# The first attention groups' rows turned, split and maximised inside the head stage of a two-layer cross-attention and expert kernel

## The reference, cut to what matters

```python
kv_dca = (y_dca @ Wkv_dca + bkv_dca)...      # last 16 context rows: own keys and values
q = _ln((x @ Wq + bq).reshape(b, s1, H, HD), qn_w, qn_b)
kv = concatenate([y_main @ Wk + bk, y_main @ Wv + bv], axis=-1).reshape(b, s2, H, 2 * HD)
k = _ln(kv[..., :HD], kn_w, kn_b);  v = kv[..., HD:]
ctx = _attn(q, k, v) + _attn(q, k_dca, v_dca)  # two softmaxes: over 496 keys and over 16
return ctx @ Wo + bo
```

## Time and profile before

| | us |
|---|---|
| median of 3 runs (2388.86 to 2392.63) | 2389.5 |
| profiled execution, its own time | 2395.94 |
| its span | 2394.2 |
| TensorE busy | 1989.2 (83%) |
| VectorE busy | 1155.8 (48%) |
| GpSimd busy | 1141.4 (48%) |
| ScalarE busy | 543.5 (23%) |

### The profile page before, as it was taken

One profiled execution on the slowest core, in us unless ns is written; L12 is line 12 of the kernel. 1 busy time (PEld: TensorE's weight loads), 2 busy tenths in 40 slices (PEclk: granted clock), 3 DMA queues, 4 the chain that ended last, 5 costly groups with the idle time before them and its releaser, 6 DMA issues.

```text
span 2394.2 us, 33404 instructions
## 1 busy us (share of the span) xinstructions
PE 1989.2 (83%) x10468; PEld 1422.6 (59%) x10469; DVE 1155.8 (48%) x2197; ACT 543.5 (23%) x1151; POOL 1141.4 (48%) x566
## 2 busy tenths in 40 slices
PE   5946887969854889999589999999999999999910
PEld 3424443424322333333379999999999999999810
DVE  2564442057673566774773444444444554443300
ACT  3221221101112444443112221122222122222100
POOL 0000000003562455563435557667666878781886
PEclk8977997979985789999789999999999999999965
DMA  3051004121125346711124435554555545543999
GB/s 111 0 147 61 18 27 162 58 80 49 63 83 174 117 163 226 237 51 41 40 88 162 182 118 167 174 159 152 161 163 163 176 160 188 177 163 90 207 158 196
DMA packets 199485, 305.96 MB, mean 128 GB/s; under 512 B 16472, under 2 KB 94808, under 8 KB 199416
## 3 DMA queue, kind: packets, MB, share of 16 engines
q1 hardware_dynamic: 141624, 187.24, 24.8%
q0 software_dynamic: 21504, 50.93, 9.4%
q10 hardware_dynamic: 36288, 66.84, 7.9%
HBM read 186.42 MB, written 118.55 MB: 127 GB/s over the span
## 4 chain that ended last, share of the span: by engine, by line
PE 41%; POOL 5%; DVE 2%; DMA 1%; issue 1%; POOLq 0%; ACT 0%; DVEq 0%
PE psum L2230 16%; PE psum L2250 8%; PE psum L2235 8%; POOL X L1954 5%; PE psum L2255 4%; PE psum L2217 3%; PE psum L2224 2%; DMA X<-d_y,f_slots 1%; DVE f_arena L1175 1%; DVE e_gu_low L2144 0%; DVE f_arena L1165 0%; DVE f_arena L1174 0%; DVE f_arena L1183 0%; DVE e_gu_low L2079 0%; POOLq L1791 0%
## 5 line engine op out<-in xcount | busy, mean ns | idle before, releaser
L2230 PE MATMUL psum<-e_gu_high,e_rowT_high 128*128 (+1 forms) x1272 | 428.0, 339 | 6.3 <-DVE e_gu_low L2144 3.8
L2230 PE MATMUL psum<-e_gu_low,e_rowT_high 128*128 (+1 forms) x1272 | 408.6, 323 | 0.0
L2235 PE MATMUL psum<-e_gu_high,e_rowT_low 128*128 (+1 forms) x1272 | 256.1, 323 | 22.0 <-DVE e_rowT_low L2034 22.0
L1973 ACT ACTIVATE e_silu<-psum 128x352 f32<-128x352 f32 x159 | 73.7, 464 | 879.4 <-PE psum L2235 873.9
L2230 PEld LDWEIGHTS psum<-e_gu_high,e_rowT_high 128*128 128x128 f32 x1272 | 240.7, 189 | 31.1 <-issue 27.0
L2230 PEld LDWEIGHTS psum<-e_gu_low,e_rowT_high 128*128 128x128 f32 x1272 | 241.6, 190 | 3.8
L2235 PEld LDWEIGHTS psum<-e_gu_high,e_rowT_low 128*128 128x128 f32 x1272 | 213.7, 189 | 22.3 <-DVE e_rowT_low L2034 22.3
L2045 DVE TENSOR_TENSOR e_midT_low<-psum,e_midT_high 128x256 fp32r<-128x256 f32 x159 | 67.5, 424 | 325.6 <-ACT e_midT_high L1982 323.4
L2250 PE MATMUL psum<-e_d_high,e_midT_high 128*128 (+3 forms) x477 | 187.7, 394 | 1.0 <-ACT e_midT_high L1982 1.0
L2250 PE MATMUL psum<-e_d_low,e_midT_high 128*128 (+3 forms) x477 | 188.4, 395 | 0.0
L1954 POOL DMA_INDIRECT X<-d_y,f_slots x96 | 148.1, 1542 | 83.3 <-DVE f_arena L2065 52.8
(11 more groups left out here) (348 smaller groups left out, 3787.6 us busy)
## 6 DMA issues: line engine op xcount, KB each, us to landing
d_sorted<-f_hs SPq DMA_DIRECT2D x32, 1048.0 KB, 9.6
e_row<-d_sorted ACTq DMA_DIRECT2D x125, 262.0 KB
d_y<-f_arena ACTq DMA_DIRECT2D x127, 256.0 KB
f_gu_in<-in_L_ffn_w_gate SPq DMA_DIRECT2D x32, 704.0 KB, 5.2
f_gu_in<-in_L_ffn_w_up SPq DMA_DIRECT2D x32, 704.0 KB, 5.1
f_d_in<-in_L_ffn_w_down SPq DMA_DIRECT2D x32, 512.0 KB
d_y<-f_hs SPq DMA_DIRECT2D x8, 1024.0 KB, 5.7
f_d_in<-in_L_ffn_w_down SPq DMA_DIRECT2D x32, 192.0 KB
```

Source lines behind the costliest of these rows:

```text
L2230: nc.tensor.matmul(bank[:, 0:M].unsqueeze(1), rowT_high[par][:, k, :], w[:, bass.ds(buffer, 1), k, at:at + M], start=(k == 0 and n == 0), ...
L2235: last = nc.tensor.matmul(bank[:, 0:M].unsqueeze(1), rowT_low[par][:, k, :], gu_high[:, bass.ds(buffer, 1), k, at:at + M], start=False, st ...
```

## The change

A new class `Scores` holds what the attention stage's preparation needs (the row tiles inside `f_gu_in` and `f_d_in`, high, low and exact tiles, `sel`, the maxima's tile of even groups, and 14 semaphores), and its methods are the old local functions. It is made ahead of `project_heads`, so that both stages can use it.

In the head stage, SyncE loads `sel` behind the affine rows, and the rows of groups 0 and 1 (both of batch 0) once it has issued batch 1's stores. In batch 3, VectorE first clears group 0's maxima and casts `sel`; TensorE turns group 0's q rows behind kv tile 1 and its k rows behind tile 2, and group 1's rows behind the first two scores; ScalarE splits group a's rows behind each of the two squares; GpSimd makes group 0's low parts ahead of the power of k and group 1's behind it; VectorE finds three maxima of group 0 between the scaling of q and that of k, and five behind it. In every batch b_o is now added to X behind the scaling of q instead of ahead of the sum of k's squares, and the keys and values are made straight from `ctxT`, without the copy `x_ctx_b`. GpSimd's loop over the batches is written out.

In the attention stage, the loads, turns, splits, low parts, scores and maxima ahead of the group loop are gone, as is the load of `sel`; VectorE clears the maxima's tile of odd groups only.

```diff
--- before.py
+++ after.py
...
+class Scores:
+
+
+    KINDS = ("q", "k")
+    PAIRS = 2 * JT
+
+    def __init__(self, nc, c, stack):
+        self.nc, self.c = nc, c
+        gu_flat = c.gu_in[:].rearrange("p k n -> p (k n)")
+        self.row = [gu_flat[:, n * 2 * S:(n + 1) * 2 * S].rearrange("p (a j d) -> p a j d", a=2, j=JT) for n in range(2)]
+        self.exact = [gu_flat[:, 4 * S:5 * S], c.d_in[:, 0, :]]
+        self.high = [far_sbuf(nc, stack, f"y_{a}_high", [P, 3, S], F32R) for a in self.KINDS]
+        self.low = [far_sbuf(nc, stack, f"y_{a}_low", [P, 3, S], F32R) for a in self.KINDS]
+        self.sel = far_sbuf(nc, stack, "y_sel", [P, 2, P], F32R)
+        self.nmax = [c.d_in[:, 2, :].rearrange("p (j n) -> p j n", j=JT)]
+        made = [nc.alloc_semaphore("y_" + n) for n in (
+            "rows_even rows_odd q_turned k_turned q_high k_high q_exact k_exact q_low k_low shifted scored max_ready sel_ready").split()]
+        self.rows_loaded, self.turned, self.high_ready, self.exact_ready, self.low_ready = [made[2 * n:2 * n + 2] for n in range(5)]
+        self.shifted, self.scored, self.max_ready, self.sel_ready = made[10:]
+        self.of_stage = made
+        self.first, self.at = c.bank[6], 4
+
+    def load_rows(self, sp, g):
+        b, hc = g // (X_H * X_HD // P), g % (X_H * X_HD // P)
+        for kind, name in enumerate(("d_xq", "d_xk")):
+            sp.dma_start(self.row[kind][:, g % 2], self.c.dram[name][b, :, hc * P:(hc + 1) * P].rearrange("(j p) d -> p j d", p=P)).then_inc(
+                self.rows_loaded[g % 2], 16)
+...
+    def find_max(self, dve, g, n):
+        dve.wait_ge(self.scored, g * self.PAIRS + n + 1)
+        banks = self.c.psum[:, self.at:self.at + 2, :]
+        to = self.nmax[g % 2][:, j, h * X_HD:(h + 2) * X_HD].rearrange("p (h e) -> p h e", e=X_HD)
+        self.nc.vector.reduce_max(to[:, :, 1], banks[:, :, S - X_LAST:S], AX.X, negate=True)
+        self.nc.vector.reduce_max(to[:, :, 0], banks[:, :, 0:S - X_LAST], AX.X, negate=True).then_inc(self.max_ready, 1)
...
-        ctx_b = sbuf(nc, stack, "x_ctx_b", [P, KC, S])
+        sel_in = sbuf(nc, stack, "x_sel_in", [P, 2, P])
...
+            sp.dma_start(sel_in[:], c.dram["i_sel"].rearrange("p (a k) -> p a k", a=2)).then_inc(sel_loaded, 16)
             for b in range(B):
                 for tile, name, ready in ((v, "d_xv", k_copied), (q, "d_xq", q_scaled), (k, "d_xk", k_scaled)):
                     sp.wait_ge(ready, (b + 1) * (JT if ready is k_copied else 1))
                     sp.dma_start(c.dram[name][b].rearrange("(j p) d -> p j d", p=P), tile[:, b % 2]).then_inc(stored[b % 2], 16)
+                if b == 1:
+
+                    sp.wait_ge(stored[0], 16 * 3)
+                    for g in range(2):
+                        early.load_rows(sp, g)
...
-            with pool.Fori(0, B) as b:
-                for a in range(2):
-                    pool.wait_ge(hvar_ready, b * 2 + a + 1)
-                    nc.gpsimd.tensor_tensor(hrstd[:, a, :], hrstd[:, a, :], c.minus_half[:, 0:JT * H],
-                                            ALU.pow).then_inc(hrstd_ready, 1)
+
+            def power(b, a):
+                pool.wait_ge(hvar_ready, b * 2 + a + 1)
+                nc.gpsimd.tensor_tensor(hrstd[:, a, :], hrstd[:, a, :], c.minus_half[:, 0:JT * H],
+                                        ALU.pow).then_inc(hrstd_ready, 1)
+
+            for b in range(B - 1):
+                power(b, 0)
+                power(b, 1)
+            power(B - 1, 0)
+            for kind in range(2):
+                early.low_part(pool, 0, kind)
+            power(B - 1, 1)
+            for kind in range(2):
+                early.low_part(pool, 1, kind)
...
+                if b == B - 1:
+
+                    dve.wait_ge(sel_loaded, 16)
+                    nc.vector.memset(early.nmax[0], 0.0)
+                    nc.vector.tensor_copy(early.sel[:], sel_in[:]).then_inc(early.sel_ready, 1)
+                    dve.wait_ge(early.sel_ready, 1)
...
+                sum_squares(b, 1)
+                finish(b, 0, q[:, par], q_scaled)
                 for j in range(JT):
 
                     t = b * JT + j
                     nc.vector.tensor_tensor(c.X[:, t, :], c.X[:, t, :], b_o[:], ALU.add)
-                sum_squares(b, 1)
-                finish(b, 0, q[:, par], q_scaled)
+                if b == B - 1:
+                    for n in range(3):
+                        early.find_max(dve, 0, n)
                 finish(b, 1, k[:, par], k_scaled)
+            for n in range(3, early.PAIRS):
+                early.find_max(dve, 0, n)
...
-                nc.scalar.copy(ctx_b[:], c.ctxT[:, b])
...
+                    if b == B - 1:
+                        for kind in range(2):
+                            early.split(act, a, kind)
...
-                                last = nc.tensor.matmul(bank, ctx_b[:, n, j * P:(j + 1) * P], main, start=(n == 0), stop=(n == KC - 1))
+                                last = nc.tensor.matmul(bank, c.ctxT[:, b, n, j * P:(j + 1) * P], main, start=(n == 0), stop=(n == KC - 1))
...
+                    if b == B - 1 and j in (1, 2):
+                        if j == 1:
+
+                            pe.wait_ge(q_copied, B * JT)
+                        else:
+                            pe.wait_ge(early.exact_ready[0], 1)
+                        early.turn_rows(pe, 0, j - 1)
+            for n in range(early.PAIRS):
+                early.scores(pe, 0, n)
+                if n < 2:
+                    pe.wait_ge(early.exact_ready[1 - n], n + 1)
+                    early.turn_rows(pe, 1, n)
...
-            for g in range(2):
-                load_rows(g)
-            sp.dma_start(sel_in[:], c.dram["i_sel"].rearrange("p (a k) -> p a k", a=2)).then_inc(const_loaded, 16)
...
-                    load_rows(g + 2)
+                    early.load_rows(sp, g + 2)
...
-            for g in range(2):
-                for kind in range(2):
-                    low_part(g, kind)
...
-            dve.wait_ge(const_loaded, 2 * 16)
-            nc.vector.memset(nmax[:], 0.0)
-            nc.vector.tensor_copy(sel[:], sel_in[:]).then_inc(sel_ready, 1)
-            dve.wait_ge(sel_ready, 1)
+            nc.vector.memset(nmax[1], 0.0).then_inc(nmax_set, 1)
+            dve.wait_ge(nmax_set, 1)
...
-            for n in range(PAIRS):
-                find_max(0, n)
...
-            for g in range(2):
-                for kind in range(2):
-                    split(g, kind)
...
+                if g == 0:
+                    pe.wait_ge(const_loaded, 16)
...
-            for g in range(2):
-                for kind in range(2):
-                    if g > 0 or kind > 0:
-                        pe.wait_ge(exact_ready[1 - kind], g + kind)
-                    turn_rows(g, kind)
-            for n in range(PAIRS):
-                scores(0, n)
...
-            for stage in (load_constants, map_attention, token_choice_ffn, project_heads):
+            for stage in (load_constants, map_attention, token_choice_ffn):
                 stage(nc, c)
                 end_stage(nc, c)
+            c.gu_in = far_sbuf(nc, stack, "f_gu_in", [P, CC, 2 * M])
+            c.d_in = far_sbuf(nc, stack, "f_d_in", [P, 3, D])
+            early = stack.enter_context(ExitStack())
+            c.scores = Scores(nc, c, early)
+            project_heads(nc, c)
+            end_stage(nc, c)
         hold_routing(nc, c, stack)
         context_attention(nc, c)
+        c.of_stage += c.scores.of_stage
         end_stage(nc, c)
+        early.close()
         routed_ffn(nc, c)
```

130 lines of the change are left out of this document (59 added, 71 removed).

## The result

The changed kernel takes 2377.5 us (median of 4 runs, 2374.9 to 2380.4), the kernel before in the same submission 2391.1 (2388.9 to 2393.8): ratio 0.9943, interval 0.9927 to 0.9959, 13.6 us less. The forecast was 2368.2, the range 2360 to 2377: right in sign, and the steps were the right ones, but the gain was forecast at 21.3 us and the time lies 0.5 us outside the range. The profiled executions, 2395.9 and 2377.1, differ by 18.9. One later run of the kernel before took 7533 us in another, slow state (granted clock 0.47) and is left out throughout.

The account below looks back on a forecast made before the run. The prediction saw a chain of waits, no engine busy, at the seam of head and attention stages. 25.4 us sooner less 4.1 for late rows gave 21.3, so 2368.2 us from the 2389.5 median; range 2360 to 2377.

Parts of the forecast that it names:

- step 7: Attention stage, group 0: group 2's rows, issued behind eleven other transfers, come late and TensorE waits; loss +4.1 us.
- step 6: Head stage's end: five maxima take 10.0 us, turnover 1.4 us; group 0's maxima are turned 25.4 us sooner.
- Steps 1 to 4: Head stage up to batch 3's power of k: effects cancel, the power starts at its old time, near 701.8.
- Step 1: Head stage, batches 0 to 2: b_o adds moved behind q's scaling let the sum of squares start sooner, -0.9 us.
- Step 2: Batch 3, VectorE's start: clearing half the maxima's tile and casting `sel` before q's bias, +0.7 us (0.5 to 1.1).
- step 3: Batch 3, TensorE: group 0's q turns fit a gap, cost 0; k turns before kv tile 3 cost +0.5 us.
- Step 5: Batch 3, VectorE: b_o adds and three maxima make the scaling of k 2.3 us late, ending at 723.8.
- The rival on the clock: Attention stage, early groups: TensorE's clock takes or gives, up to 14 us more gained; chance 0.10.
- No effect: Attention stage: a wait with its own time takes the gain back, 2389.5 us; chance 0.05.
- Slower: Groups 5 to 15 and expert stage: clock granted later or falling more often, deciding from 43 us; chance 0.04.

Follow-up runs that it names:

- the gap kernel: Rows first, plus batch 3's memset, cast and X adds put into VectorE's wait ahead of kv tile 3: 2367.1 us, ratio 0.9892.
- rows first: Changed kernel with group 2's two row tiles issued as the attention stage's first transfers: 2363.8 us, ratio 0.9877; repeated 2363.1 us, ratio 0.9872.
- the held pair: Kernel before and changed kernel, each with unread matmuls added ahead of the sums of groups 0 to 4: 2387.6 and 2369.8 us.
- the warm kernel: Rows first, plus unread matmuls filling TensorE's waits between group 0's first scores: 2375.8 us, ratio 0.9931.
- the delay: The gap kernel plus 2.7 us of useless VectorE clearing between the scaling of k and the last five maxima: 2368.5 us, ratio 0.9906.

## Why the prediction was wrong in size, and what it had right

The forecast gain was 21.3 us, the one shown beside it 13.6, and the better measured one 16 to 18. The mechanism held: the preparation moved, and the only wait that took part of it back is the one of step 7. The steps that failed are terms of the sum:

- step 7, the late rows: 4.1 us forecast, 5.8 to 5.9 measured, since the second row tile landed after 4.8 us and not after 2.8;
- steps 1 and 3, which left TensorE's clock in kv tile 2 out (put at nothing): 1.8 us, 0.7 of them in batch 1 and 1.1 in batch 3;
- the turnover of step 6, 0.5 too long, which went the other way.

Together the steps take 3 us from the forecast gain. The rest of the distance from 2368.2 to 2377.5 is 1.6 us because the forecast was taken from a median of 2389.5 of three runs where the kernel before then had 2391.1, and some 4 to 5 us that belong to no step. In detail:

- **Steps 1 to 4** were to cancel and cost 1.8 us (the power of k started 1.8 later against the head stage's first transposes). Step 1 brought 0.3 in batch 0 and 0.3 in batch 2, but in batch 1 kv tile 2 took 6.08 us instead of 5.40, so that by the sum of batch 2 only 0.25 of its 0.9 was left. Step 2's 0.7 is 0.8. In batch 3 a later bias add widens TensorE's gap ahead of kv tile 2: the gap moves tile 2 to 1.2 GHz, 1.1 us (4.78 against 3.70). I had the clock's price in step 3, but for the transposes alone, not for the work behind the gap. Shown by the gap kernel, where both went away together (1.9 us). The copy `x_ctx_b` that I put at 0 is part of the gap: without it TensorE waits 2.25 us instead of 3.19 for the turned rows ahead of each batch's q, so it is 0.9 us further ahead of VectorE and then waits longer.
- **Step 5**: 2.3 us late forecast, 2.1 measured. Right, yet I counted the delay as pure loss. It also avoids the contention with group 1's low parts, some 2 us; removing one without the other gave 0.3.
- **Step 6**: five maxima took 10.0 us as forecast; the turnover 0.9 instead of 1.4. The maxima were turned 24.3 us sooner, 25.4 forecast.
- **Step 7** named the wait and its place, and was mis-sized: 6.49 us of wait less 0.57 of slack is 5.9 instead of 4.1, and group 0 grew by 5.8 (5.2 with the clock held). The loads were issued when I had said (6.05 us after the stage's start); the second row tile landed 4.8 us after its issue. I took the shortest landing, 2.8, although in my own sum 1.65 MB stood ahead of it. The median, 6.2, was nearer. The rule of the Trainium skill quoted under step 7 is about the order in which an engine takes up descriptors, and the changed kernel agrees with the use I made of it: w_o, issued at 739.90, landed after 5.8 us, ahead of both row tiles. It is no rule of completion: with rows first, w_o, issued at 742.75, landed after 8.2 us, and the gate's weights, issued 0.5 later, after 5.6.
- **The sum** so becomes 24.3 - 5.9 = 18.4 us, which the held pair shows as 17.8. My 21.3 was 3 us too high by steps.
- **The other 4 us** (17.8 less 13.6) are no step, and that they came out on this side was chance: the other runs gave 17.8 for the same pair. Time in groups 1 to 5 and 14 follows patterns of TensorE's clock that differ between executions of one program. The rival on the clock was half right: the clock does give or take several us. But the groups did not run as the later ones (116.8 us for groups 1 to 5, 118.8 before), and the warm kernel shows that the clock at the stage's entry is worth 0.8 us.
- **The range** failed by 0.5 us since I took the spread of three runs (3.8 us) for the kernel's. It is 13.6 over 69 runs, so a median of four is itself uncertain by some 2 us (an estimate from the spread of the 69). "0.2% can be told" was too bold.
- *No effect* and *Slower* did not happen: no stage behind took the gain back, and groups 6 to 13 kept their 1.00.

What stays open: what picks the pattern. Not the stage's start alone (the delay), not the waits as the trace shows them (the gate's two rows, group 14). The Trainium skill, TensorE: Matmul & The Clock Gate, section Part 1: The HAM clock gate, calls the time at the low clock at a kernel's start variable from run to run; that fits two patterns of one program, but no run here shows the cause.

## What to carry to other kernels

When work moves ahead of a stage boundary, look at once at the next load behind it in the queue's order: two issues moved to the front gave 12 us beside the 16 of the whole change, 6.3 of them by the wait that went and the rest by a better pattern of the clock. Price a gap of TensorE by the work behind it, not by the gap, and check that a delay you remove is not what keeps VectorE and GpSimd apart. Where one program's runs fall into two groups, no difference under their distance is told by a few medians; make that part cost the same in both kernels, or compare traces stage by stage, and look into two traces of one program before you explain a difference.

## What the runs showed of the hardware

- GpSimd's subtraction of 128x512 and VectorE's multiply of two SBUF operands stretch each other (1.26 to 3.31 us, 2.29 to 3.35); beside maxima from PSUM the subtraction stays at 1.26. GpSimd's power, 12.5 us, stretched nothing.
- Eight records (four matmuls of 512 columns) behind a wait of TensorE: 3.70 us behind 0.81, 2.05 and 2.88 us of idle, 5.40 behind 3.26 and 3.88, 6.51 behind 3.48, 6.08 behind 4.49. With four transposes in the gap: 4.78 behind 2.28 us, the transposes and 0.1 (3.5 in all), and 3.70 behind 1.47, the transposes and 0.54. The time at 1.2 GHz does not follow the length of the gap alone.
- In group 14 of the changed kernel the clock fell although TensorE had not waited longer than 0.65 us at a time; in another kernel it stayed at 1.00 behind the same waits.
- A matmul of 512 f32 columns shows as two records that follow each other every 0.43 us at 2.4 GHz and every 0.85 at 1.2.
- The same instructions behind the same idle took 5.91 and 3.62 us, by when the clock came back; which of the two followed the program in all 18 traces.
